# First attention's score operands in two 64-row halves of a tile, and its last row of maxima sent before the second attention's first load

## The reference, cut to what matters

```
x  = layernorm(x)
# first attention: 16 heads of width 8, rotary positions, causal
q, k, v = split(xn @ qkv_w.T + qkv_b); q, k = rope(q), rope(k)
s = q @ k.T / sqrt(8);  s = where(key > query, -max, s)
a = (softmax(s) @ v) @ out_w.T + out_b
# second branch: six nodes c, each an attention of 8 heads of width 16, no mask
q = ew[c,0] * (nodes[c-1] @ We + be)         # k and v from earlier nodes
nodes[c] = act_w[c] * mha(q @ Wq, k @ Wk, v @ Wv) + q
out = x + a + layernorm(nodes[5]) * g + b
```

## Time and profile before

| | |
|---|---|
| median of three runs | 1427.39 us |
| the profiled execution | 1423.05 us, of which the span of its instructions 1421.3 us |
| TensorE busy | 1380.5 us (97%) |
| DVE busy | 1263.0 us (89%) |
| ACT busy | 1139.5 us (80%) |
| chain that ended last | PE 88%, DMA 4%, DVE 3% |
| first matmul of a score | 37.87 us after the start |
| steps of A with both score passes | from about 55 to 266 us |

### The profile page before, as it was taken

One profiled execution on the slowest core, in us unless ns is written; L12 is line 12 of the kernel. 1 busy time (PEld: TensorE's weight loads), 2 busy tenths in 40 slices (PEclk: granted clock), 3 DMA queues, 4 the chain that ended last, 5 costly groups with the idle time before them and its releaser, 6 DMA issues.

```text
span 1421.3 us, 60282 instructions
## 1 busy us (share of the span) xinstructions
PE 1380.5 (97%) x26216; PEld 935.3 (66%) x26216; DVE 1263.0 (89%) x1587; ACT 1139.5 (80%) x2133; POOL 449.8 (32%) x936
## 2 busy tenths in 40 slices
PE   6899999999999999999999999999999999999995
PEld 4467777656667666676676766766667666667652
DVE  8889999999989989899899898988989989989895
ACT  3378887688878878888788887887888878878784
POOL 5141115324422433233423332234233432330210
PEclk9899999999999999999999999999999999999998
DMA  8131112343232422333323323233233332321211
GB/s 253 47 116 60 51 59 98 119 142 119 81 127 70 132 97 77 102 109 107 104 78 114 107 74 121 83 123 107 69 101 107 101 107 80 127 98 56 76 38 40
DMA packets 115668, 137.68 MB, mean 97 GB/s; under 512 B 14972, under 2 KB 90109, under 8 KB 115277
## 3 DMA queue, kind: packets, MB, share of 16 engines
q1 hardware_dynamic: 115405, 133.83, 28.7%
HBM read 64.63 MB, written 61.98 MB: 89 GB/s over the span
## 4 chain that ended last, share of the span: by engine, by line
PE 88%; DMA 4%; DVE 3%; SPq 2%; ACT 1%; POOL 1%; issue 1%; ACTq 0%; POOLq 0%; DVEq 0%
PE s L1069 53%; PE cps L1163 26%; PE misc L1069 7%; DMA qs<-mrows 2%; DVE neg_max L971 1%; SPq L431 1%; PE misc L1064 1%; ACT probs L784 1%; DMA dram_raw_b<-csb 1%; PE s L1064 0%; DVE s L967 0%; POOL parts L601 0%; POOL ks L596 0%; POOL full L614 0%; SPq L500 0%
## 5 line engine op out<-in xcount | busy, mean ns | idle before, releaser
L784 ACT ACTIVATE probs<-s 128x512 f32<-128x512 f32 x1792 | 1059.2, 599 | 227.4 <-PE s L1069 166.8
L971 DVE TENSOR_REDUCE neg_max<-s 128x1 f32<-128x1024 f32 x768 | 936.5, 1222 | 62.0 <-PE s L1069 9.1
L1069 PE MATMUL s<-qs,ks 99*32 99x512 bf16 (+2 forms) x7680 | 808.4, 370 | 7.1 <-DMA qs<-mrows 5.1
L1069 PE MATMUL s<-ks,qs 96*32 96x512 bf16 (+2 forms) x7680 | 606.5, 369 | 6.3 <-DMA ks<-dram_qk_a 2.7
L1163 PE MATMUL cps<-probs,vs 128*32 128x256 f32 (+1 forms) x7552 | 591.4, 368 | 0.6 <-ACT probs L784 0.6
L1069 PEld LDWEIGHTS s<-qs,ks 99*32 99x32 bf16 x7680 | 235.8, 94 | 240.6 <-ACT probs L784 96.7
L1163 PEld LDWEIGHTS cps<-probs,vs 128*32 128x32 f32 x7552 | 316.4, 110 | 76.3 <-issue 17.0
L1069 PEld LDWEIGHTS s<-ks,qs 96*32 96x32 bf16 x7680 | 292.5, 97 | 88.6 <-issue 24.5
L633 POOL TENSOR_TENSOR mparts<-neg_max,zeros 128x8 bf16<-128x8 f32 x128 | 26.0, 203 | 796.0 <-DVE neg_max L971 654.3
L967 DVE CUSTOM_DVE_ANT_0 s<-s,mask_q 128x1024 f32<-128x1024 f32 (+7 forms) x256 | 187.8, 785 | 23.5 <-PE s L1069 14.8
L706 POOL TENSOR_TENSOR parts<-full,zeros 128x512 bf16<-128x512 f32 x48 | 61.4, 1280 | 52.2 <-DVE full L949 52.2
(11 more groups left out here) (134 smaller groups left out, 607.6 us busy)
## 6 DMA issues: line engine op xcount, KB each, us to landing
dram_qk_b<-parts SPq DMA_DIRECT2D x48, 384.0 KB, 3.2
qs<-dram_qk_b SPq DMA_DIRECT2D x96, 192.0 KB
ks<-dram_qk_b SPq DMA_DIRECT2D x96, 192.0 KB
dram_qk_b<-parts SPq DMA_DIRECT2D x48, 256.0 KB, 3.2
dram_raw_b<-csb SPq DMA_DIRECT2D x93, 128.0 KB, 4.3
dram_qk_b<-parts SPq DMA_DIRECT2D x48, 128.0 KB, 3.2
vsrc<-srcT SPq DMA_DIRECT2D x12, 512.0 KB, 3.1
ctx_b<-dram_raw_b SPq DMA_DIRECT2D x44, 128.0 KB
```

Of the source, the lines that this page charges most:

```text
L784: nc.scalar.activation(buf[:, lo:hi], s2[bank][:, 0:hi - lo], ACT.Exp, scale=scale).then_inc(exp_done, 1)
L971: last = ve.tensor_reduce(peak, scores, AX.X, ALU.max, negate=True)
L1069: last = te.matmul(dst[c0:c0 + STRIP, :], lhsT[:, c0:c0 + STRIP], rhs, start=start, stop=stop, tile_position=(0, c0))
```

## The change

The operands of A get tiles of their own: `qa`, two new tiles, and `ka`, two bfloat16 views of the halves of `ctx_b`, which is free until B's contexts are read. Head k of A uses tile k % 2, in rows 0 to 47 when k % 4 is 0 or 1 and in rows 64 to 111 when it is 2 or 3. Its rows of maxima are the three behind (48 to 50 or 112 to 114). The score matmuls of A are now of 48 or 51 rows, placed at row 0 or 64 of the array. In one step, head k's first scores and head k-2's second scores have the same tile and opposite halves. The mask's matmul uses the same 64 rows; because a half of an identity reaches only 64 keys, the two strips in the other half take a shifted mask (`mask_far`). The products and their results stay what they were. B is as before.

```diff
+ROWS_A = 6 * DA
+HALF_ROWS = 64
+        ka = [ctx_b[:, n * CH:(n + 1) * CH].bitcast(BF16) for n in range(2)]
+        def first_row(which, k):
+            return HALF_ROWS * (k % RING // 2) if which == "A" else 0
+        def operands(which, k):
+            return (qa[k % 2], ka[k % 2]) if which == "A" else (qs[k % RING], ks[k % RING])
+        def data_rows(which, k):
+            row = first_row(which, k)
+            return slice(row, row + (ROWS_A if which == "A" else KROW))
...
-                    if k == UP - 1 and kind not in ("BE", "T"):
+                    if k == UP - 1 and kind not in ("AZ", "BE", "T"):
                         load_unit(kind, r, UP, b)
                     if kind_at(kind, k, 1):
                         sp.wait_ge(mrow_sb, u)
-                        sp.dma_start(qs[(k - 1) % RING][MROW:KALL, :].rearrange("a (i n) -> a i n", n=128),
+                        sp.dma_start(operands(which, k - 1)[0][max_rows(which, k - 1), :
...
+                    if kind == "AZ" and k == UP - 1:
+                        load_unit(kind, r, UP, b)
...
+            for s in range(RING):
+                pool.wait_ge(pool_const, 8 + s)
+                pl.memset(ks[s][MROW:128, :], 1.0).then_inc(pool_const, 1)
+            pool.wait_ge(pool_const, 8 + RING)
             for n in range(NB):
                 pool.wait_ge(ln_stats, n + 1)
...
+            for mask, key_of_row_0 in ((mask_k, 0), (mask_far[0], HALF_ROWS), (mask_far[1], -HALF_ROWS)):
...
             for s in range(RING):
-                for ring in (qs[s][:, :], ks[s][:, :], vs[s][:, :, :]):
-                    ve.memset(ring, 0.0).then_inc(dve_const, 1)
+                ve.memset(vs[s][:, :, :], 0.0).then_inc(dve_const, 1)
+            for n in range(2):
+                ve.memset(ka[n][:, :], 1.0).then_inc(dve_const, 1)
...
-            def mm_strips(dst, lhsT, rhs, start=True, stop=True):
+            def mm_strips(dst, lhsT, rhs, start=True, stop=True, row=0):
                 for c0 in range(0, 128, STRIP):
                     last = te.matmul(dst[c0:c0 + STRIP, :], lhsT[:, c0:c0 + STRIP], rhs, start=start, stop=stop,
-                                     tile_position=(0, c0))
+                                     tile_position=(row, c0))
+            def mask_strips(dst, row):
+                rows = slice(row, row + HALF_ROWS)
+                for c0 in range(0, 128, STRIP):
+                    here = c0 // HALF_ROWS == row // HALF_ROWS
+                    at, mask = (c0, mask_k) if here else ((c0 + HALF_ROWS) % 128, mask_far[row // HALF_ROWS])
+                    last = te.matmul(dst[c0:c0 + STRIP, :], ident_h[rows, at:at + STRIP], mask[rows, :],
+                                     start=False, stop=True, tile_position=(row, c0))
```

More of the change, by code:

```diff
@@ L197 @@
 FINISH = [(0, TB)] + [(TB + t0, tiles) for t0, tiles in LATE_TILES]
-N_CONST = 12 + 2 * RING
+N_CONST = 20 + RING
 def added(kind, r, k):
@@ L273, in dual_attention_kernel @@
         mask_k = sb("mask_k", [128, 128], BF16)
+        mask_far = [sb(f"mask_far{n}", [128, 128], BF16) for n in range(2)]
+        qa = [sb(f"qa{n}", [128, S], BF16) for n in range(2)]
         ones_row = sb("ones_row", [1, 128])
@@ L567, in _ @@
             pl.memset(mask_q[:, :], 0.0).then_inc(pool_const, 1)
-            pl.memset(mask_k[:, :], 0.0).then_inc(pool_const, 1)
-            pool.wait_ge(pool_const, 3)
+            for mask in (mask_k, *mask_far):
+                pl.memset(mask[:, :], 0.0).then_inc(pool_const, 1)
+            pool.wait_ge(pool_const, 5)
             pl.affine_select(out=ident[:, :], in_=ident[:, :], pattern=[[-1, 128]], compare_op=ALU.not_equal,
@@ L1277, in score_piece @@
                 which = kind_at(kind, k, 2)
-                q, ky = qs[(k - 2) % RING], ks[(k - 2) % RING]
+                q, ky = operands(which, k - 2)
+                rows, row = score_rows(which, k - 2), first_row(which, k - 2)
                 lo, hi = pieces(which, j)[n]
@@ L1287, in score_piece @@
                     diagonal = which == "A" and first == at
-                    last = mm_strips(bank[:, first - lo:end - lo], ky[0:KALL, t * 128:(t + 1) * 128],
-                                     q[0:KALL, q0 + first - at:q0 + end - at], stop=not diagonal)
+                    last = mm_strips(bank[:, first - lo:end - lo], ky[rows, t * 128:(t + 1) * 128],
+                                     q[rows, q0 + first - at:q0 + end - at], stop=not diagonal, row=row)
                     if diagonal:
-                        last = mm_strips(bank[:, at - lo:at - lo + 128], ident_h[:, :], mask_k[:, :],
-                                         start=False)
+                        last = mask_strips(bank[:, at - lo:at - lo + 128], row)
                 last.then_inc(s2_ready, 1)
@@ L1309, in phase @@
                         if kind != "T":
-                            q, ky = qs[k % RING], ks[k % RING]
+                            q, ky = operands(kind[0], k)
+                            rows, row = data_rows(kind[0], k), first_row(kind[0], k)
                             if i == 0:
@@ L1320, in phase @@
                                         continue
-                                    last = mm_strips(s1[n % 2][:, lo:hi], q[0:KROW, t * 128:(t + 1) * 128],
-                                              ky[0:KROW, lo - at:hi - at])
+                                    last = mm_strips(s1[n % 2][:, lo:hi], q[rows, t * 128:(t + 1) * 128],
+                                                     ky[rows, lo - at:hi - at], row=row)
                             last.then_inc(s1_ready, 1)
```

29 lines of the change are left out of this document (17 added, 12 removed).

## The result

The changed kernel takes 1435.13 us (median of 8 runs, 1431.35 to 1438.43), the one before, timed beside it, 1427.70 us (8 runs, 1426.09 to 1431.25). The ratio is 1.0052, interval 1.0039 to 1.0064: slower by about 7.4 us, where 1416 us was forecast. The profiled executions are 12.5 us apart (1435.52 and 1423.05), so the profile shows some 5 us more of loss than the medians do.

A forecast was written before the change was run, and what follows sets the result against it. TensorE was taken to set A's pace, DVE close behind. Gains of 10.4 (steps), 0.4 (start) and 0.8 us (end of AZ) made 11.6 us, from the median 1427.39 to 1415.8, said as 1416 us; range 1410 to 1446.

The forecast's parts named there:

- The border of A and B: End of AZ: row of maxima sent 0.8 us earlier, B's loads later; 0.8 us gained, ends 1.7 gained, 0.9 lost.
- its own first term: A's 29 steps: 0.36 us saved per step, 10.4 us in all.
- The halves: A's score matmuls in opposite row halves run side by side: step from 6.51 to 6.15 us, 10.4 us over 29 steps.
- p: Price of a pair of changes between 64-row and 128-row work on TensorE: taken as 0.05 us, bounds 0 and 0.35.
- the break-even of 0.145: Price in us of a pair of row changes at which A's step stays at 6.51 us.
- the nearer row: Trace row taken as guide for the price: 24 to 32 columns costs nothing, against 0.35 us at the full-array matmul.
- the walk: Turn-by-turn count of A's step with only neighbouring matmuls overlapping: 0.82 us saved per step before the floor and row changes.
- its floor: ACT's exponential loop in A: 1.25 us from a two-piece turn's first piece to the next turn's.
- The start: Before A: POOL's fills leave, two short masks come in; 0.4 us gained, ends 1.0 gained, 0.6 lost.
- Rival 1: Row changes in A's 29 steps are dear, p 0.2 to 0.35: 1432 to 1450 us; chance 0.22.
- Rival 3: Halves in A don't run side by side: 1426 us with cheap changes, 1438 us and more otherwise; chance 0.13.

The follow-up runs named there:

- the filled wait: The changed kernel with five groups of float32 strip matmuls on constants put ahead of TensorE's wait for B's first head: 1427.22 us, ratio 1.0002.
- the early operands: The changed kernel with B's first projections one step of AZ earlier and B head 0's load at the head of step 7: 1421.80 us, ratio 0.9961.
- the row-0 kernel: The changed kernel with all heads of A in rows 0 to 63 of their own tiles, so nothing runs side by side: 1471.82 us, ratio 1.0310.
- the 48-row run: The kernel before, with only the first scores of A0's heads 0 and 1 taking 48 rows in place of 96: 1429.68 us, ratio 1.0019.

## Why the prediction was wrong, step by step

**The border of A and B: the step that failed.** The prediction put it as "I take 0.8 us gained; ends: 1.7 gained, 0.9 lost". Measured from head 30 to head 33: 14.3 us lost (15.1 less the 0.8 of the moved mark). The step held the old end of A (265.4 us) against the new landing times. But its own first term moves A: TensorE came 3.6 us earlier, while the last transfer landed 1.2 us earlier. It also let the loads take 3 to 4.3 us; `ks` took 6.05. These two make 2.4 us more of waiting. The rest, 11.9 us, was not in the text at all: after the wait the clock was granted at 1.2 GHz for 22 us. That the clock carries at least 7.3 us is shown by the filled wait; that the whole loss is the border's, and not the halves', by the early operands, which turn 7.4 us lost into 5.6 gained.

**The halves: the sign was right, the size by luck.** -0.36 us a step was forecast, -0.20 measured in the step shown, and -6.3 us from head 2 to head 30, where 28 x 0.36 = 10.1 were due. Two errors, one of +0.72 us a step (6.85 for 6.13) and one of -0.54 (6.31 for 6.85), nearly cancel. First, p: taken at 0.05, measured at 0.23 in the row-0 kernel, above the break-even of 0.145 that I had worked out. I took the change of columns for the nearer row; it is a change of rows that costs. The Trainium skill's rule that I weighed and set aside (TensorEngine Tiling (Array Packing), "Key Properties": a change of mode drains the array) agrees with the row-0 kernel's trace in that TensorE stands at such a change, and the measured price is 0.10 us in and 0.13 out. Second, the walk: "TensorE starts its work in order, so only neighbours overlap". The first matmul of the other half starts ahead of a mask that stands before it. (The Trainium skill, TensorE: Matmul & The Clock Gate, "The mechanism", has matmuls start strictly in program order, as I did; across row halves the rows at 163.14 and 163.34 say otherwise, and the measurement decides.) With p at 0.23 and turn 0 at its floor the walk gives 1.59, 1.48, 1.43, 1.10 and 1.25 us for turns 1, 2, 3, 4 and 0, 6.85 in all; the trace has 1.48, 1.23, 1.43, 0.95 and 1.22. Turns 1, 2 and 4 are where it fails. Saved side by side: 1.30 us measured, where the walk at this p gives 7.61 - 6.85 = 0.76.

**The start**: 0.4 us gained was forecast; the first score matmul came at 37.77 us, inside the 37.0 to 37.9. But I followed only the path up to it. Behind it the clock stays low 14 us longer, 2.5 us lost at head 2, and the 48-row run shows that fewer rows in two heads' first scores bring most of this.

**Rivals.** Rival 1 (changes are dear) had p right and the reason for the loss wrong: its 29 steps did not lose anything. Rival 3 fell: the halves do run side by side. None of the three named the clock. The range held the time because rival 1's time happened to lie there.

**What stays open.** Behind a wait of 1.9 us at the border the half clock lasts 3.4 us with full rows and about 20 with A's few rows; whether the rows or the changes of rows do it was not shown. Nor was what decides whether it falls at all: with full rows it fell behind 1.93 and 1.90 us and not behind 1.70 and 2.63. Of the 2.0 us that the profile loses after head 33 and of where the early lead at the start goes I have no row.

## What to carry to other kernels

A faster loop arrives earlier at what follows it: hold the next transfers against the *new* time of arrival, and issue them early enough before the loop is made faster. Packing small matmuls in row halves pays only if what it saves side by side exceeds 0.23 us for each place where full-row work stands between; gathering those places helps only while the turns left over are not held by another engine. And at the start and at the border of A and B the clock was late to rise in every profile here that had small-row work at that place, so look at the granted clock behind every wait, not only at the busy share.

## What the runs showed of the hardware

- Matmuls of 64 and of 128 rows in turn cost TensorE 0.23 us for each pair of changes (0.10 in, 0.13 out); 1.10 us in a step with five (7.61 us for 6.51).
- Two groups in opposite row halves run side by side (163.11 and 163.14), and the second starts ahead of an earlier mask (163.34) of the first half.
- Being busy is not enough for the clock to rise. With the same matmuls in 48 in place of 96 rows it rose at 59 us in place of 48.7, TensorE being busy 7.66 of the 8 us from 48 on. In the row-0 kernel, busy 18.00 of 18 us, it stayed at 0.50 until 82 us.
- Behind a wait of 1.9 us at the border the clock fell to 1.2 GHz both with few rows (1.92 and 1.86 us) and with full rows (1.93 and 1.90), and in another run with full rows it stayed at 2.4 GHz through 2.63 us. It was back after about 3.4 us with full rows and after about 20 with A's 51-row groups among B's. Float32 matmuls on constants in the wait held it up.
